# The order of four interleaved recurrences in a one-core kernel: the LSTM behind the delta rule on every engine, the RNN's product at the end of the step

## What is computed

```python
# LSTM over x, started from cond
z = xz_t + prev_h @ Wh;  i, f, o = sigmoid(...);  g = tanh(...)
next_c = f * prev_c + i * g;  next_h = o * tanh(next_c)
# delta rule over the LSTM's output, 8 heads of 32, state S of 32 x 32 per head
kn = k / (norm(k) + 1e-6);  delta = v - S @ kn
S = tanh(beta * S + delta * kn^T);  Sq = S @ q;  out = Sq * silu(Sq)
x = x + out @ W_out
# plain RNN over the new x, started from cond
next_h = tanh(prev_h @ Wh + x @ Wx + b)
```

## Time and profile before

| | us |
|---|---|
| median of 3 runs (3473.26 to 3475.56) | 3473.64 |
| the profiled execution's own time | 3478.83 |
| its span, first to last instruction | 3477.0 |
| PE busy in the span | 2897.3 (83%) |
| DVE busy | 1842.8 (53%) |
| ACT busy | 1110.5 (32%) |
| POOL busy | 761.8 (22%) |
| mean granted TensorE clock (1 is 2.4 GHz) | 0.641 |

### The profile page before, as it was taken

The page is one execution under the profiler, slowest core; times in us unless marked ns, Lnnn a source line. Parts: engine busy times, 40 slices in busy tenths (PEclk is TensorE's granted clock), DMA queues, the critical chain, the costliest instruction groups (busy, mean ns, idle before and its releaser), DMA issues. The chain is left out here.

```text
span 3477.0 us, 94868 instructions
## 1 busy us (share of the span) xinstructions
PE 2897.3 (83%) x35915; PEld 2164.5 (62%) x35915; DVE 1842.8 (53%) x7177; ACT 1110.5 (32%) x4414; POOL 761.8 (22%) x1477
## 2 busy tenths in 40 slices
PE   6899999956888894689899899888547789999998
PEld 3557888844555663456666666665314578888755
DVE  3534444464435433456656656654375854444577
ACT  1233222221222232334444444443223432222222
POOL 1111111102200001344544544545101211111000
PEclk9996555556997795555555555555558955555699
DMA  1000000000000001343343343343000000000000
GB/s 74 2 2 0 0 0 0 0 33 1 2 2 0 1 0 58 66 98 71 66 98 71 66 98 71 65 98 71 37 0 1 2 0 0 0 0 0 0 0 12
DMA packets 106860, 101.37 MB, mean 29 GB/s; under 512 B 95616, under 2 KB 95616, under 8 KB 97536
## 3 DMA queue, kind: packets, MB, share of 16 engines
q1 hardware_dynamic: 106624, 98.13, 12.9%
HBM read 89.68 MB, written 8.39 MB: 28 GB/s over the span
## 5 line engine op out<-in xcount | busy, mean ns | idle before, releaser
L574 POOL TENSOR_TENSOR l2r_beta_s<-l2r_state,l2r_beta_f 128x256 f32<-128x256 f32 x512 | 360.5, 725 | 543.8 <-ACT l2r_state L479 528.5
L695 DVE TENSOR_TENSOR l2r_pre<-l2r_o_ps,l2r_beta_s 128x256 f32<-128x256 f32 x512 | 193.4, 419 | 246.0 <-PE l2r_o_ps L374 245.9
L479 ACT ACTIVATE l2r_state<-l2r_pre 128x256 f32<-128x256 f32 x512 | 190.7, 417 | 260.0 <-DVE l2r_pre L695 260.0
L327 PEld LDWEIGHTS l2r_lstm_ps<-l2r_h_ring,l2r_w_part 128*128 128x128 bf16 x3072 | 103.6, 105 | 222.4 <-DVE l2r_h_low L681 220.9
L362 PE MATMUL l2r_d_ps<-l2r_state,l2r_kq 128*32 128x128 f32 x2056 | 206.8, 421 | 36.4 <-ACT l2r_state L479 36.3
L327 PE MATMUL l2r_lstm_ps<-l2r_h_ring,l2r_w_part 128*128 128x8 bf16 x3072 | 123.4, 169 | 121.7 <-DVE l2r_h_low L681 121.7
L374 PE MATMUL l2r_o_ps<-l2r_rows,l2r_outer 32*128 32x128 f32 x2048 | 207.8, 496 | 15.9 <-DVE l2r_rows L687 15.9
L469 ACT ACTIVATE l2r_lstm_ps<-l2r_lstm_ps 128x24 f32<-128x24 f32 x256 | 44.8, 175 | 392.0 <-PE l2r_lstm_ps L327 391.9
L340 PEld LDWEIGHTS l2r_r_ps<-l2r_r_ring,main_even_layers 128*128 128x128 f32 x512 | 128.8, 311 | 59.3 <-issue 47.1
L340 PE MATMUL l2r_r_ps<-l2r_r_ring,main_even_layers 128*128 128x8 f32 x512 | 149.3, 365 | 9.7 <-ACT l2r_r_ring L487 9.7
L133 PE MATMUL l3r_acc<-l3r_xw,main_base 128*128 x512 | 154.7, 389 | 1.6 <-issue 1.6
(11 more groups left out here) (534 smaller groups left out, 7565.1 us busy)
## 6 DMA issues: line engine op xcount, KB each, us to landing
l2r_beta_f<-l2r_beta_store SPq DMA_DIRECT2D x256, 256.0 KB, 6.1
main_odd_layers<-in_l SPq DMA_DIRECT2D x1, 4826.5 KB, 14.3
l2r_beta_store<-l2r_beta_tok SPq DMA_DIRECT2D x256, 8.0 KB, 1.5
main_odd_layers<-in_l SPq DMA_DIRECT2D x1, 3672.0 KB, 16.0
l2r_v_store<-l2r_v_part SPq DMA_DIRECT2D x128, 24.0 KB, 2.0
l2r_v_rows<-l2r_v_store SPq DMA_DIRECT2D x16, 192.0 KB, 6.3
main_decay<-in_decay SPq DMA_DIRECT2D x1, 3072.0 KB, 11.3
main_even_layers<-in_l SPq DMA_DIRECT2D x1, 2762.5 KB, 9.3
```

Source lines behind the costliest of these rows:

```text
L327: last = nc.tensor.matmul(lstm_ps[:, at + g * B:at + (g + 1) * B], w_part[k][:, g * P:(g + 1) * P], h, start=False, stop=(m == 2), skip_gr ...
L479: nc.scalar.activation(state[:, h * 2 * P:(h + 1) * 2 * P], pre[:, h * 2 * P:(h + 1) * 2 * P], ACT.Tanh).then_inc(state_ready[h], 1)
L574: nc.gpsimd.tensor_tensor(beta_s[:, half], state[:, half], beta_f[:, q % BETA_SLOTS, n % QUARTER, half], ALU.mult).then_inc(s["bs_ready"], 1)
L695: nc.vector.tensor_tensor(pre[:, half].rearrange("p (c n) -> p c n", c=2), o_ps[:, 2 * h:2 * h + 2, 0:P], beta_s[:, half].rearrange("p (c ...
```

## The change

All of it lies in `recurrent_stages`.

1. **PE's order.** The spread of the delta comes directly behind the retrieval; behind it, at step 0, the RNN's inputs, the LSTM's bias and its four input products; then the LSTM's products, then the RNN's product, then the pieces of `project` and `output` and the values.
2. **ACT's order.** The RNN's tanh first, then the new state, then the LSTM's gates and tanh.
3. **DVE's order.** The output sum of step 0 comes ahead of the masked copy. The LSTM's h of the step before and its split come behind the masked copy, then the sums, then the pieces of `project` and `output`, last the LSTM's cell.
4. **The LSTM alone.** Up to token 31 (IN_BANK, the bodies without a delta rule) h is made and split at once, in SBUF, by two operations; the products take the high half of `h_rest` for the middle part of h and wait for each part by itself.

```diff
+        IN_BANK = 2 * TC - 1
...
                 def lstm_products(n):
                     at = n % TC * 4 * B
-                    pe.wait_ge(s["low_ready"], n + 1)
-                    for m, h in enumerate((high(h_ring[:, (n - 1) % SLOTS, :]), h_mid[:, :], h_low[:, :])):
+                    alone = n <= IN_BANK
+                    if not alone:
+                        pe.wait_ge(s["low_ready"], n + 1)
+                    h_parts = high(h_ring[:, (n - 1) % SLOTS, :]), high(h_rest[:, :]) if alone else h_mid[:, :], h_low[:, :]
+                    for m in range(3):
+                        if alone:
+                            pe.wait_ge(s[("h_ready", "rest_ready", "low_ready")[m]], n + 1)
                         for g in range(4):
                             for k in range(3 - m):
...
                         if delta is not None or final:
                             retrieve(n)
-                        if lstm is not None and lstm >= 1 and step == 0:
-                            lstm_bias(lstm)
-                            lstm_inputs(lstm, 0)
-                        elif lstm is not None:
-                            lstm_products(lstm * TC + step)
                         if delta is not None:
                             spread_delta(n)
-                        if lstm is not None and lstm >= 1 and step == 0:
-                            for g in range(1, 4):
-                                lstm_inputs(lstm, g)
-                            lstm_products(lstm * TC)
+                        if rnn is not None and step == 0:
+                            rnn_inputs(rnn)
+                        if lstm is not None:
+                            if lstm >= 1 and step == 0:
+                                lstm_bias(lstm)
+                                for g in range(4):
+                                    lstm_inputs(lstm, g)
+                            lstm_products(lstm * TC + step)
                         if rnn is not None:
-                            if step == 0:
-                                rnn_inputs(rnn)
                             rnn_product(rnn * TC + step)
...
-                        if lstm is not None:
-                            lstm_gates(lstm * TC + step)
+                        if rnn is not None:
+                            rnn_tanh(rnn * TC + step)
                         if delta is not None:
                             new_state(delta * TC + step)
                         if lstm is not None:
+                            lstm_gates(lstm * TC + step)
                             lstm_tanh(lstm * TC + step)
-                        if rnn is not None:
-                            rnn_tanh(rnn * TC + step)
...
+                def split_alone(n):
+                    h = h_ring[:, n % SLOTS, :]
+                    dve.wait_ge(s["h_ready"], n + 2)
+                    nc.vector.tensor_tensor(h_rest[:, :], h, high(h), ALU.subtract).then_inc(s["rest_ready"], 1)
+                    dve.wait_ge(s["rest_ready"], n + 2)
+                    nc.vector.tensor_tensor(h_low[:, :], h_rest[:, :], high(h_rest[:, :]), ALU.subtract).then_inc(s["low_ready"], 1)
...
+                        if rnn is not None and step == 0:
+                            add_out(rnn)
                         if delta is not None or final:
                             masked(n)
-                        if rnn is not None and step == 0:
-                            add_out(rnn)
+                        before = k * TC + step - 1
+                        if IN_BANK <= before < T:
+                            lstm_h(before)
+                        if IN_BANK <= before < T - 1:
+                            split_h(before)
+                        if delta is not None:
+                            summed(n)
                         if proj is not None:
                             project(proj, step)
                         if out is not None:
                             output(out, step)
-                        if delta is not None:
-                            summed(n)
                         if lstm is not None:
-                            lstm_cell(lstm * TC + step)
-                            lstm_h(lstm * TC + step)
-                        if lstm is not None and lstm * TC + step + 1 < T:
-                            split_h(lstm * TC + step)
+                            lstm_cell(before + 1)
+                            if before + 1 < IN_BANK:
+                                lstm_h(before + 1)
+                                split_alone(before + 1)
```

More of the change, by code:

```diff
@@ L247, in recurrent_stages @@
         h_ring = mem.sb("h_ring", [P, SLOTS, B])
-        h0_rest, h_mid, h_low = mem.sb("h0_rest", [P, B]), mem.sb("h_mid", [P, B], BF16), mem.sb("h_low", [P, B], BF16)
+        h_rest, h_mid, h_low = mem.sb("h_rest", [P, B]), mem.sb("h_mid", [P, B], BF16), mem.sb("h_low", [P, B], BF16)
         w_part = [mem.sb(f"w_part{n}", [P, 4 * P], BF16) for n in range(3)]
@@ L280, in recurrent_stages @@
         names = ("consts_ready", "w_split", "bias_split", "bias_psum", "bias_ready", "xw_psum", "gates_psum", "gates_ready", "mul_ready",
-                 "cell_ready", "tanh_ready", "h_ready", "h_psum", "rest_psum", "mid_h_ready", "low_ready", "xin_psum", "xp_sig_ready", "xp_ready",
+                 "cell_ready", "tanh_ready", "h_ready", "rest_ready", "h_psum", "rest_psum", "mid_h_ready", "low_ready", "xin_psum", "xp_sig_ready", "xp_ready",
                  "kv_psum", "kv_ready", "bq_psum", "beta_in", "q_ready", "k_sq_ready", "ssq_ready", "norm_ready", "inv_ready",
@@ L322, in lstm_products @@
                     at = n % TC * 4 * B
-                    pe.wait_ge(s["low_ready"], n + 1)
-                    for m, h in enumerate((high(h_ring[:, (n - 1) % SLOTS, :]), h_mid[:, :], h_low[:, :])):
+                    alone = n <= IN_BANK
[5 more added lines that the diff above has]
+                            pe.wait_ge(s[("h_ready", "rest_ready", "low_ready")[m]], n + 1)
                         for g in range(4):
                             for k in range(3 - m):
-                                last = nc.tensor.matmul(lstm_ps[:, at + g * B:at + (g + 1) * B], w_part[k][:, g * P:(g + 1) * P], h,
-                                                        start=False, stop=(m == 2), skip_group_check=True)
+                                last = nc.tensor.matmul(lstm_ps[:, at + g * B:at + (g + 1) * B], w_part[k][:, g * P:(g + 1) * P],
+                                                        h_parts[m], start=False, stop=(m == 2), skip_group_check=True)
                     last.then_inc(s["gates_psum"], 1)
@@ L662, in lstm_h @@
                     at = n % TC * 4 * B
-                    out_gate = lstm_ps[:, at + 2 * B:at + 3 * B]
                     dve.wait_ge(s["tanh_ready"], n + 1)
@@ L772, in _ @@
                 nc.vector.tensor_copy(selv_bf[:, :], sel_v).then_inc(s["consts_ready"], 1)
-                dve.wait_ge(s["h_ready"], 1)
-                nc.vector.tensor_tensor(h0_rest[:, :], h0, high(h0), ALU.subtract).then_inc(s["mid_h_ready"], 1)
-                dve.wait_ge(s["mid_h_ready"], 1)
-                nc.vector.tensor_copy(h_mid[:, :], high(h0_rest[:, :]))
-                nc.vector.tensor_tensor(h_low[:, :], h0_rest[:, :], high(h0_rest[:, :]), ALU.subtract).then_inc(s["low_ready"], 1)
+                split_alone(-1)
                 for k in range(BODIES + 1):
```

14 lines of the change are left out of this document (8 added, 6 removed).

## The result

| | before | after |
|---|---|---|
| median of the runs, us | 3473.45 (4 runs, 3472.09 to 3475.56) | 3518.40 (4 runs, 3517.21 to 3522.87) |
| the profiled execution's own time | 3478.83 | 3519.45 |
| its span | 3477.0 | 3517.7 |
| first gates to last masked copy (body 18) | 1327.39 to 2450.17: 1122.8 | 1315.10 to 2492.51: 1177.4 |
| one of bodies 4 to 15, mean | 65.6 | 71.1 |

The changed kernel takes 1.013 times as long (95% interval 1.0116 to 1.0144), 45 us more. Measured again (e11) it was 1.0155 (1.0141 to 1.0169), 52 us more.

The account below looks back on a forecast made before the run. The prediction took a repeating chain of waits, not busy PE, as the bound. Its terms, 47 - 16 - 9 + 4 = +26 us, put the median at 3500 us from 3473.64 (+0.75%), range 3482 to 3518.

Parts of the forecast that it names:

- bodies 0 and 1: LSTM alone: step from 2.78 to 2.02 us, 21 steps counting, the rest lost to a DMA wait; -16 us.
- bodies 2 and 3: LSTM and delta, no RNN: steps of 3.26 us, then a DMA wait; 121.4 against 130.8 us, -9 us.
- bodies 4 to 15: All four waves: 15 x 4.10 + 6.9 + 1.1 = 69.5 us a body against 65.6; +47 us.
- bodies 16 and 17: State waits 1.52 us behind the spread instead of 1.33 (+3); v rows later (+1); +4 us.
- The full step: Bodies 4 to 15: new state waits for the RNN's tanh and product; about 4.10 us against 3.93.
- the rival with early loaded weights: RNN's weights load under the LSTM's last products, step 3.90 us, 3463 us in all; chance 0.13.
- the LSTM's tanh: Rival: it comes too late, so h, split and products slip 0.2 us in 180 steps; 3536 us, chance 0.10.
- The clock: Rival: PE's clock rises from 1.2 to 2.4 GHz, saving about 190 us; 3310 us, chance 0.01.
- Pieces: Projection and output work on DVE, ACT, POOL fits idle time; uncovered remainder 1.1 us per body.
- two table loads: Step 6, around the square root: two loads of 1.28 us on ACT, delaying the RNN's tanh by 0.4 us.
- Step 0: First step of a body: RNN's product 4.67 us behind the masked copy, state at 5.45, step 6.9 us.
- busy PE is no bound here: Reading of the kernel before: PE busy 59.7 of 66 us, but a chain of waits repeats and bounds.

Follow-up runs that it names:

- e11: The changed kernel as it is, measured once more; median 3526.10 us, 1.0155 of before.
- e2: Changed kernel with ScalarE's order only altered: new state, LSTM gates, RNN tanh, LSTM tanh; median 3455.82 us, 0.9948 of before.
- e1: Changed kernel plus a one-column sigmoid right behind the square root and, in step 12, the output's cell turned ahead of the sums; 3506.76 us, 1.0096 of before.
- e6: Kernel of e5 plus the two repairs of e1 and, at step 0, the RNN's inputs between retrieval and spread; 3432.48 us, 0.9883 of before.
- e5: Changed kernel, RNN's product between retrieval and spread from step 1, at step 0 inputs and product directly behind the spread; 3453.11 us, 0.9942 of before.
- e8: Changed kernel with the v rows' load ahead of the first beta load on SP's queue; 3518.57 us, 1.0137 of before.
- e3: Changed kernel with PE's order only altered: RNN's product directly behind the spread, ahead of the LSTM's products; 3460.89 us, 0.9967 of before.
- e7: Kernel of e6 with the v rows' load ahead of the first beta load on SP's queue; 3381.55 us, 0.9731 of before.
- e9: Kernel before the change with the v rows' load ahead of the first beta load on SP's queue; 3470.72 us, 0.9987 of before.
- e10: Kernel of e7 with DVE's product with the sigmoid in step 2 of the projections ahead of the sums; 3374.95 us, 0.9715 of before.

## Why the forecast was wrong

The direction and the mechanism held, the size did not. Term by term, on the stage (us):

| term | forecast | measured |
|---|---|---|
| bodies 0 and 1 | -16 | -15.4 |
| bodies 2 and 3 | -9 | -4.2 |
| bodies 4 to 15 | +47 | +65.7 |
| bodies 16 and 17 | +4 | +8.6 |
| sum | +26 | +54.6 |

- **The full step** (15 x 4.10) was right: 4.07, and the state is held by the RNN's product (e2: 3.25 without). The weight load (1797.12) came 0.64 us behind the start of the LSTM's products, as in the earlier trace rows, so the rival with early loaded weights fell; the LSTM's tanh (1799.26) was in time for h behind the masked copy, so that rival fell too. The clock stayed at 0.50.
- **The step that failed is "Pieces"**, 1.1 us a body where 2.8 were measured. What it counted was sized well: the square root with two loads 0.4 (4.51 - 4.07 in e1), the projections 0.45 (0.19, 0.13 and 0.13 in steps 2, 3 and 5). But "two table loads" were taken over from the trace of before as if the number did not depend on what follows the square root. The order that put the RNN's tanh first made a third, 1.23 us (e1). And DVE's pieces were priced at nothing "while that idle time lasts": idle time on DVE covers the engine's own work, not the wait of PE for the transposed cell, 0.49 us (e1). Twelve times 1.72 is 20.6 us. Bodies 4 to 15 missed by 18.7 in all, because plain steps at 4.07 instead of 4.10 took 5.4 back while step 0 added 4.2. The whole stage missed by 28.6.
- **Step 0**, 6.9 against 7.25. PE's weight load for the RNN came 5.00 us behind the masked copy (1599.48 - 1594.48) and not 4.67. The forecast named this loss of up to 0.3 for the lost cover, but set the same size of gain against it. No gain came. That the lost cover is the reason is argued and not isolated by a run; e6, which puts the RNN's inputs under the masked copy, has a step 0 that is 0.27 shorter than e5's. (The 4.67 is the start of the weight load, the product itself began at 4.88; in the new order the two start within 0.02 us, so the sum took no harm from that.) Twelve times 0.35 is 4.
- **Bodies 2 and 3**: 121.4 us were foretold and 126.7 measured. Steps 0 to 6 of body 2 took 29.2 us and not 27.5, because step 6 lasted 5.0 (the third load again) and step 2 4.26; so the kn tile was ready 32.0 and 32.1 us into the two bodies and not 30.4. From then on the DMA chain decided, as foretold, and it took 31.0 and 29.8 us where 28.9 to 29.5 were foretold. In e1, with two loads, the bodies are 63.1 and 61.9 instead of 63.9 and 62.8, but e11 shows that they vary by 0.9 together in the same kernel. In e8, with the v rows early, body 2 is 3.8 us shorter.
- **Bodies 16 and 17.** Steps of 3.43 instead of 3.25 in 17 of 32, as the 0.74 + 0.63 + 0.15 and the count of 18 said: 3 us. Not in the sum were the late transposition (4.58 in step 12 where before had 3.45, twice 1.1), the two steps 0 (0.9 together) and step 2 of body 16 (0.7). The wait for the v rows cost 1.8 and not 1 in this execution and nothing in e11, so that the +8.6 is +6.8 there; this term is no larger than the variation from one execution to the next.
- **The reading that bounded too little:** "busy PE is no bound here". True of the kernel before and of plain steps. In seven of the 16 steps (2, 3, 5 and 12 to 15) PE's packed work was, after the change, as long as the chain of waits or longer, so there the wait for the product cost nothing more. It did not spoil the sum, whose step lengths with pieces were estimated close; but it spoiled the forecasts of the repairs, as the expectations of e2 and e3 show.
- **The table loads.** The Trainium skill's figures (ScalarE: Activation LUTs, What ACT_TABLE_LOAD costs) are 1283 ns for a load and 1380 ns of drain. The changed trace has three loads and again no drain: from the load at 1624.04 to its tanh are 1.30 us, and the load itself comes 0.02 us behind the square root's end. The Trainium skill (ScalarE activation tables: per-element evaluation and per-set limits, the section on table sets in the compiler and the runtime) says further that within a block loads are placed greedily, for the longest run that a set can serve. By that a set with tanh and sigmoid would be loaded behind the square root, and step 6 would have two loads; the trace has three, and the measurement decides.

The stages ahead gave 12 us back in the first profile, which nothing in the change explains; by e11 (3526.1 against 3474.5) the change costs 52 us. So the 45 us of the first measurement, and with it how near the forecast came, owe something to chance.

## What to carry to other kernels

A forecast of a new order needs the order of functions on ScalarE beside that of times: ask at each switch which set the first function behind it will load, and whether the next function is in it; if not, one small activation of the right kind in front can spare a load: here it cost 0.11 us and saved one of 1.28, 1.23 us of a body. And compare every chain of waits with each engine's packed work, step by step: where PE loses the work that covered a copy on another engine, the second bound moves up, and work put under that copy (here the RNN's product, which needs nothing of the step) brings it down: 4.20 to 3.78 us in steps 3 and 5 (e5). When the steps have become shorter, look at once at the transfers that end a wave: here a load's place on its queue was worth 50 us of the stage in e7, and 4 in the kernel before (e9).

## What the runs showed of the hardware

- A load of 192 KB landed 6.5 us after its issue (median) when four beta loads stood directly ahead of it on SP's queue, and 3.0 us when they stood behind it (e6, e7). The same edit gave 6.4 and 3.2 us on the changed kernel (e8), 6.3 and 3.2 on the one before (e9).
- After the square root the set of tables loaded for a tanh did not serve the sigmoid (a load of 1.28 us at L473 in the changed kernel); the one loaded for a sigmoid served both.
- With PE busy in 710.5 of 724.0 us (e10, bodies 4 to 15) the granted clock was 0.50 but for two short stretches at 1.00 (around 1589 and 1951 us); e3, e6 and e7 have one such stretch each in those bodies. In the kernel before and the changed one it was 0.50 over all of bodies 4 to 15, with PE busy in 90% and 83%.
- The same stages ahead of this one ended anywhere within 16 us from execution to execution, with granted clocks of 0.72 (e3) to 0.80 (changed, e2) in one and the same window of the trace.
